# Moving one quad's copy, two tiles' normalisation and a send of weights between engines

## What is computed

```python
def _layernorm(x, g, b):
    m = x.mean(-1, keepdims=True)
    v = ((x - m) ** 2).mean(-1, keepdims=True)
    return (x - m) / jnp.sqrt(v + 1e-05) * g + b
def _attn(q_in, k_in, v_in, wq, bq, wk, bk, wv, bv, wo, bo, causal):
    ...
    scores = jnp.einsum('bqhd,bkhd->bhqk', Q, Kp) / jnp.sqrt(jnp.float32(HD))
    ...
    a = jax.nn.softmax(scores, axis=-1)
    o = jnp.einsum('bhqk,bkhd->bqhd', a, V).reshape(Bq, Sq, Dm)
    return o @ wo + bo
def _moe(x, rw, rb, w1, b1, w2, b2):
    router_weights = jax.nn.softmax(xf @ rw + rb, axis=-1)
    topw, topi = jax.lax.top_k(router_weights, K)
    ...
    out = jnp.einsum('etd,te->td', eo, combine)
x = _layernorm(x + _attn(x, x, x, ..., True), ln1_g, ln1_b)
x = _layernorm(x + _attn(x, encoder_output, encoder_output, ..., False), ln2_g, ln2_b)
x = _layernorm(x + _moe(x, router_w, router_b, e_w1, e_b1, e_w2, e_b2), ln3_g, ln3_b)
```

## Time and profile before

| | us |
|---|---|
| median of 3 runs | 758.14 |
| lowest, highest | 756.41, 762.37 |
| the profiled execution | 757.34 |
| its span in the profile | 755.6 |
| TensorE busy in it | 712.6 (94%) |
| VectorE busy | 498.8 (66%) |
| ScalarE busy | 369.4 (49%) |
| GpSimd busy | 286.9 (38%) |

### The profile page before, as it was taken

One profiled execution on the slowest core, in us unless ns is written; L12 is line 12 of the kernel. 1 busy time (PEld: TensorE's weight loads), 2 busy tenths in 40 slices (PEclk: granted clock), 3 DMA queues, 4 the chain that ended last, 5 costly groups with the idle time before them and its releaser, 6 DMA issues.

```text
span 755.6 us, 14560 instructions
## 1 busy us (share of the span) xinstructions
PE 712.6 (94%) x4969; PEld 478.9 (63%) x4969; DVE 498.8 (66%) x1376; ACT 369.4 (49%) x749; POOL 286.9 (38%) x558
## 2 busy tenths in 40 slices
PE   6889999999999999999997899999999999999983
PEld 4444434545464454645563586898999999999941
DVE  5679787678766877656668654465666665666436
ACT  4325465665666676667753446433433333333403
POOL 8305521543653463624653333212332332232114
PEclk9999999999999999999987999999999999999997
DMA  8964421343164021316016873677999999999654
GB/s 273 291 145 129 118 95 46 84 129 128 33 180 127 13 60 49 91 39 183 14 62 216 251 254 98 210 254 239 346 328 342 342 330 338 345 330 336 231 186 164
DMA packets 95154, 140.29 MB, mean 186 GB/s; under 512 B 11855, under 2 KB 81077, under 8 KB 92597
## 3 DMA queue, kind: packets, MB, share of 16 engines
q1 hardware_dynamic: 76357, 107.86, 45.3%
q10 hardware_dynamic: 15072, 22.02, 8.9%
q0 software_dynamic: 3648, 9.45, 3.4%
HBM read 110.65 MB, written 28.65 MB: 184 GB/s over the span
## 4 chain that ended last, share of the span: by engine, by line
PE 76%; DVE 8%; issue 8%; DMA 4%; POOL 2%; ACT 1%; DVEq 0%; SPq 0%; ACTq 0%; POOLq 0%
PE out_acc L984 12%; PE score_pair L961 10%; PE work L932 9%; PE score_pair L855 8%; PE work L849 8%; PE work L906 6%; PE work L855 4%; PE work L1008 4%; DVE neg_part_max L1472 3%; PE score_pair L849 3%; PE work L918 2%; PE work L992 2%; PE work L935 2%; DMA arena<-parts_scratch 1%; PE work L872 1%
## 5 line engine op out<-in xcount | busy, mean ns | idle before, releaser
L1472 DVE TENSOR_REDUCE neg_part_max<-work 128x1 f32<-128x512 f32 (+4 forms) x368 | 213.2, 625 | 66.8 <-PE work L935 36.1
L1244 ACT ACTIVATE arena<-score_pair 128x1024 f32<-128x1024 f32 (+2 forms) x224 | 178.7, 839 | 76.9 <-PE score_pair L961 75.7
L932 PE MATMUL work<-arena 96*128 96x77 bf16 (+4 forms) x640 | 118.2, 277 | 10.7 <-ACT arena L1207 2.7
L984 PE MATMUL out_acc<-arena 128*32 128x512 f32 (+4 forms) x896 | 103.7, 517 | 2.6 <-DVE arena L1492 2.6
L961 PE MATMUL score_pair<-arena 99*128 99x512 bf16 (+2 forms) x448 | 103.9, 337 | 1.0 <-ACT arena L1244 1.0
L1904 POOL DMA_INDIRECT chosen_scratch<-arena,scatter_rows x36 | 35.6, 989 | 174.8 <-DVE arena L1404 174.5
L855 PE MATMUL score_pair<-arena 128*128 128x256 f32 x432 | 97.6, 379 | 0.0
L932 PEld LDWEIGHTS work<-arena 96*128 96x128 bf16 x640 | 49.2, 98 | 74.7 <-issue 30.7
L1960 POOL TENSOR_SCALAR_AFFINE_SELECT arena<-arena 128x256 f32<-128x256 f32 x128 | 51.5, 410 | 118.0 <-ACT arena L1244 116.8
L1177 ACT ACTIVATE arena<-work,expert_b_cols 128x128 f32<-128x128 f32 x180 | 51.1, 369 | 84.2 <-PE work L849 79.4
L849 PE MATMUL work<-arena 128*128 128x128 f32 x720 | 87.2, 278 | 0.1
(11 more groups left out here) (257 smaller groups left out, 958.2 us busy)
## 6 DMA issues: line engine op xcount, KB each, us to landing
arena<-in_L_xattn_e_w SPq DMA_DIRECT2D x54, 1024.0 KB, 6.8
arena<-parts_scratch SPq DMA_DIRECT2D x24, 768.0 KB, 6.0
arena<-in_L_xattn_e_w ACTq DMA_DIRECT2D x18, 1024.0 KB
parts_scratch<-arena_more SPq DMA_DIRECT2D x24, 384.0 KB, 2.6
parts_scratch<-arena_more SPq DMA_DIRECT2D x24, 256.0 KB, 3.0
parts_scratch<-arena_more SPq DMA_DIRECT2D x24, 128.0 KB, 3.0
residual<-in_x SPq DMA_DIRECT2D x4, 512.0 KB, 8.0
tokens_scratch<-residual SPq DMA_DIRECT2D x2, 1024.0 KB, 4.8
```

What stands on the lines that cost most here:

```text
L932: m = pe.matmul(bank[:, j * it.w:(j + 1) * it.w], qa[st.half(it.g)][0:R_S, h, n0:n0 + P], k, start=True, stop=not it.last)
L984: m = pe.matmul(o_ps[c * VW:(c + 1) * VW, skip:QG], v, pt[buf][0:rows, j, 0:QG - skip], start=first, stop=last)
L1244: act_e.activation(pt[buf][0:rows, :, 0:w], st2[pair][0:rows, :, 0:w], ACT.Exp, scale=float(HD) ** -0.5).then_inc(pair_taken[pair], 1)
L1472: dve.tensor_reduce(pm[:, it.at, it.t, it.h0:it.h0 + it.nh], bank[:, 0:it.nh * it.w].rearrange("p (j k) -> p j k", j=it.nh), AX.X, ALU.max ...
```

## The change

Three things change; nothing else does.

1. A function `taken_by_scalar` decides who copies a quad. It differs from before for one quad: quad 0 of stage 7, half 0, is copied by ScalarE and no longer by VectorE.
2. A function `applied_by_pool` decides who normalises a tile. It differs from before for tiles 5 and 7 of sequence 1 after self-attention: ScalarE and GpSimd do them, in three instructions, and no longer VectorE, in two. TensorE's transposes of these two tiles wait for `normal_g` and no longer for `normal_v`; the counts that SyncE waits for at the end are adapted.
3. In `ORDER`, the `t_weights` of tile 0 (B) moves from before `w_exp` (X) to after that quad's `weigh` and `normalise`.

```diff
-    "R2q2M2Hewq2f2awlqsnqf2Pan2wn2q2n2Kywqfnf2qwfa2SRvhwuMRMRdMRMHt2yq2otoqtzwuvPKo2qSedwuq2Fq2BXwuawax2Oa2xBkxId"
+    "R2q2M2Hewq2f2awlqsnqf2Pan2wn2q2n2Kywqfnf2qwfa2SRvhwuMRMRdMRMHt2yq2otoqtzwuvPKo2qSedwuq2Fq2XwuBawax2Oa2xBkxId"
...
+def applied_by_pool(it):
+
+    return it.b == 0 or not it.cross and it.t in (5, 7)
+
+
+def taken_by_scalar(it):
+
+    return (it.g + it.quad) % 2 == 1 or (it.st.n, it.g) == (7, 0)
...
-            apply_n[it.cross, it.b, it.t] = sum(z.b == it.b for z in find("out_apply")[:it.n]) + 1
+            apply_n[it.cross, it.b, it.t] = sum(applied_by_pool(z) == applied_by_pool(it) for z in find("out_apply")[:it.n]) + 1
...
-        N_APPLY = 2 * TB
+        apply_at = {(it.cross, it.b, it.t): it.n for it in find("out_apply")}
+        N_BY_POOL = sum(applied_by_pool(it) for it in find("out_apply"))
+        N_BY_VECTOR = len(find("out_apply")) - N_BY_POOL
...
-            return (normal_v if b else normal_g, apply_n[cross, b, t])
+            by_pool = applied_by_pool(find("out_apply")[apply_at[cross, b, t]])
+            return (normal_g if by_pool else normal_v, apply_n[cross, b, t])
...
-                elif it.kind == "normalise" and (it.g + it.quad) % 2:
+                elif it.kind == "normalise" and taken_by_scalar(it):
...
-                elif it.kind == "out_apply" and it.b == 0:
+                elif it.kind == "out_apply" and applied_by_pool(it):
...
-                elif it.kind == "normalise" and (it.g + it.quad) % 2 == 0:
+                elif it.kind == "normalise" and not taken_by_scalar(it):
...
-                elif it.kind == "out_apply" and it.b == 1:
+                elif it.kind == "out_apply" and not applied_by_pool(it):
...
-                elif it.kind == "out_apply" and it.b == 0:
+                elif it.kind == "out_apply" and applied_by_pool(it):
...
-                    sp.wait_ge(normal_g, N_APPLY + (n + 1) * PIECE)
+                    sp.wait_ge(normal_g, N_BY_POOL + (n + 1) * PIECE)
                 else:
-                    sp.wait_ge(normal_v, N_APPLY + 1)
+                    sp.wait_ge(normal_v, N_BY_VECTOR + 1)
```

## The result

| | before | after |
|---|---|---|
| median of 18 runs each, us | 758.87 (756.41 to 765.10) | 763.34 (759.82 to 766.06) |
| ratio to before, with its 95% interval | 1 | 1.0052 [1.0036, 1.0069] |
| the profiled execution, us | 757.34 | 765.91 |
| its span, us | 755.6 | 764.2 |
| TensorE busy in it, us | 712.6 | 716.8 |

The change costs 2.7 to 5.2 us (the interval times 758.87). That is within 1%, and 763.34 lies inside the forecast range of 757.0 to 763.5, 0.2 under its upper end; the forecast was 760.1, a loss of about 2.4 us. The profiled execution of after is not a typical one: it lies 2.6 us above the median of its kernel. So the two spans, 8.6 us apart, must not be subtracted to get the price of the change.

What follows compares the result with a forecast made beforehand. TensorE bounds the kernel; copy, sends and tiles form one chain delaying the projection by 2.35 us, rounded to 2.4, giving 759.7 from the profiled execution or 760.5 from the median; forecast 760.1 us, range 757.0 to 763.5.

Steps and rivals of the forecast that it cites:

- The copy: Quad 0 of stage 7: ScalarE copies behind `w_exp` at about 407.4, so TensorE starts the next quad 0.35 us later.
- The sends: Two weight issues on ScalarE follow the copy, at 408.1 and 409.2; their lateness itself is priced at nothing.
- The tiles: Tiles 5 and 7 take 2.21 us each over ScalarE and GpSimd, against 1.00 on VectorE; tile 7's transposes +2.35 us.
- Tile 6: Before its transposes: VectorE has its data ready since 409, its two operations ending before tile 5 reaches GpSimd.
- GpSimd stretched: Rival at tiles 5 and 7: both GpSimd multiplies slowed by VectorE work, +0.86 us, so 761.0; chance 0.06.
- The clock: TensorE's granted clock, at its lower level from 405 us, came back at about 416, some 1.1 us into the projection.
- bounds of -0.5 and +2.7: Projections: gain about 0.5 us if the clock returns no later than before, +2.7 if only after both.
- The rival in which it lags through both projections: TensorE's clock stays at the lower level until both projections end: 760.1 + 2.7 = 762.8 us; chance 0.10.
- still at half behind 419: Sign that the forecast is wrong: TensorE's granted clock remains at half after 419 us.
- Behind the projection: Parts go out to HBM in 3.33 us and back in 5.51, unchanged, so the maxima are late with the projection.
- The early copy: Rival: ScalarE copies the quad at 405.1, projection gains 0.5 to 0.8 at full clock, 756.6 to 757.4; chance 0.12 shared with swallowed delay.
- likeliest case: The main forecast, projection and end 2.4 us late, 760.1 us, alone spanning 758.8 to 761.4; chance 0.69.

Runs made afterwards that it cites:

- copy alone: Kernel before with only the quad's copy moved to ScalarE; median 759.00 us, ratio 0.9992 [0.9968, 1.0017].
- sends back: Changed kernel with the two sends of weights put back ahead of `w_exp` on ScalarE; median 759.31 us, ratio 1.0023 [0.9994, 1.0052].
- copy early: Changed kernel with `w_exp` put behind the quad's copy and the sends behind `w_exp`; median 762.91 us, ratio 1.0055 [1.0034, 1.0076].
- everything early: Changed kernel with the copy, ScalarE's parts of tiles 5 and 7 and the sends all ahead of `w_exp`; median 758.71 us, ratio 0.9984 [0.9953, 1.0015].
- lean version: Changed kernel with copy, then sends, `w_exp` behind the last tile's transposes, all four tiles on VectorE; median 758.35 us, ratio 0.9998 [0.9976, 1.002].
- second set: The changed kernel run and profiled again with no edit; median 760.81 us, ratio to the kernel before 1.0034 [1.0015, 1.0053].
- tiles with sends: Changed kernel with the quad's copy back on VectorE; median 763.11 us, ratio 1.0041 [1.0016, 1.0065].
- only tile 5: Changed kernel with tile 7 back on VectorE, tile 5 staying on ScalarE and GpSimd; median 759.51 us, ratio 1.0002 [0.9976, 1.0028].
- copy with sends: Changed kernel with tiles 5 and 7 back on VectorE; median 760.32 us, ratio 1.0001 [0.9971, 1.0032].
- sends alone: Kernel before with only the two sends of weights moved behind `w_exp` and the quad; median 759.20 us, ratio 1.0013 [0.999, 1.0037].

## Why the prediction was right

**The copy.** Forecast: behind `w_exp`, 3.4 us after the start of the sums, with TensorE 0.35 us later than before. Measured: 3.33 (408.28 - 404.95) and +0.26; the copy took 0.57 us for the assumed 0.59, and started 0.11 us after the start of the second exponential instead of 0.17. This was the mechanism that the prediction turned on, and the trace has it as forecast. The copy alone gave +0.24 at tile 7.

**The sends.** Forecast from neighbours: first issue 0.68 us after the copy's start, the second 1.12 later. Measured: 0.77 and 1.12. The next instruction then follows 0.44 us after the second issue's start, so tile 5 starts 5.66 us behind the sums where the forecast had 5.3 to 5.6. It does not begin before the issue ends (0.39 us), as the lower bound had assumed.

**The tiles** were the term that was mis-sized. The price of 2.21 us (2.20 with the 0.72 that the earlier trace rows has for the add) ended with GpSimd's add and left out the hand-over to TensorE, 0.15 us; and tile 5's add took 0.80 instead of 0.72 or 0.73. From ScalarE's start to the transposes it was 413.04 - 410.61 = 2.43 us for tile 5 and 416.36 - 414.00 = 2.36 for tile 7. So TensorE waited 1.58 us before tile 5, not 1.1, and 1.73 before tile 7, not 1.6. Tile 5's transposes came at 8.09 for a forecast of 7.75 (+0.34), tile 7's at 11.41 for 11.03: +2.73 us against +2.35. The runs with one part undone show that it is this chain: with the sends back 1.82 us of it are gone, with tile 7 back on VectorE 1.94, and with the quad's copy early none of it but 0.18.

**Tile 6** was misread. The prediction has VectorE ready with it since 409, and its two operations over before tile 5 reaches GpSimd. But in VectorE's order the copy of tile 4's transposes stands ahead of tile 6, in the kernel before as well; the pair at 408.46 and 408.98 is tile 5's. The timeline of before, at 410 us:

```profile
410.28 0.42 DVE L1427 COPY arena_more<-work 128x256 f32<-128x256 f32 x1 [0.82 <-PE work L872]
...
410.62 0.47 DVE L1526 SCALAR_TENSOR_TENSOR residual<-residual,mean_var,param_rows 128x256 f32<-128x256 f32 x1
```

In the changed kernel the two operations of tile 6 ran at 411.83 and 412.35, right beside GpSimd's work on tile 5. This cost nothing, because they ended at 413.18 and TensorE came to tile 6 at 413.96.

**GpSimd stretched.** The rival's price went to the wrong engine. No GpSimd operation here took over 0.80 us; VectorE's were stretched instead, L1542 by 0.35 us (0.83 for 0.48) and L1720 by 0.40 (0.57, against 0.17 in the runs where no GpSimd instruction is beside it). SBUF — State Buffer of the Trainium skill (SBUF: two separate sides) states an exclusive lock between a GpSimd operation and a VectorE operation that has two SBUF inputs or runs in a 2-port mode: whichever starts first has it for its whole length, and the other is blocked. On VectorE's side the traces agree: L1720 ended at 416.24 and GpSimd's add at 416.21, L1542 at 413.18 and the add beside it at 412.89. On GpSimd's side they show less: its add at 412.09 took 0.07 us longer than usual, though VectorE's L1539 had begun before it and ran until 412.31. In the changed kernel this costs nothing: tile 6 waits for tile 5 and `rows` in TensorE's order anyway. In the version with everything early it held VectorE by 0.53, 0.47 and 0.35 us ahead of tile 4, of the 1.5 us by which tile 4 came later than expected.

**The clock.** The forecast kept the projection at its old length, with bounds of -0.5 and +2.7. It took 2.84 us for 2.48. The granted clock of the changed kernel, TensorE alone, from 417 us and from the start of the projection:

```profile
417.00:421.00 4.00, 4.00 (x13) 0.57 1.05 380
```

```profile
418.52:422.12 3.60, 3.60 (x11) 0.73 1.09 364
```

0.73 stands against 0.83 before. The maxima are 0.36 us later than tile 7's delay alone gives (3.09 - 2.73), which is the projection's 0.36. So the clock came back later than before by more than the work was moved, by a little, and neither bound was reached. The rival in which it lags through both projections did not happen. But one of the prediction's own signs of being wrong did: a granted clock "still at half behind 419". A mean of 0.57 from 417 to 421 us means the lower level until about 420.4, or 419.5 less the 0.95 us of offset. The clock came back 1.9 us into the first projection instead of 1.2; the second took 1.88 us, as before. So the sign came, and the large loss that it stood for did not. In the second execution of the changed kernel the clock came back 15.0 us behind the start of the sums instead of 15.5, the projection took 2.57 us, and the maxima were 2.61 us late.

**Behind the projection.** Forecast 3.33 + 5.51 us for the parts; 3.25 + 5.60 came, and TensorE's last wait, 1.31 us, is as before. The statement that a microsecond lost before the projection is a microsecond of the kernel fits the losses: +2.6 and +3.1 us at the maxima, 2.6 and 3.9 us by the ratios (0.34% and 0.52% of 759). For gains it was not seen: the lean version starts its projection 1.53 us earlier and its time cannot be told from before.

**The early copy** as a rival was priced at 756.6 to 757.4 if it happened. It did not happen, as forecast, and the lean version, where the copy is early, speaks against the price: 1.53 us of lead at the projection, 0.57 at the maxima, nothing in the time that the runs can tell ([-1.8, +1.5] us, which does not exclude it). In its trace the step that fails is "with the clock kept up the projection gains 0.5 to 0.8": the clock was not kept up (0.52), and the projection lost 1.1.

**How much of the hit is luck.** The place of the loss, its releasers and its size within 0.4 us at tile 7 were forecast. The time was not met as closely. The measured 763.34 lies above the likeliest case (758.8 to 761.4), and inside the range only through the room left for a clock that lags through both projections, which did not happen. Of the 3.2 us above the forecast, 1.1 are the kernel before, which the forecast took at 757.7 (between 757.34 and 758.14) and which was measured at 758.87; 0.4 are the tiles and 0.4 the projection. The remaining 1.4 or so are not traced to a place; the mean granted clock of the runs, 0.978 in this set and 0.980 in the second, hints at the clock and shows no more. The second set's 760.81 lies within the likeliest case.

**Open.** In the time from the parts' store to its landing there are two groups: 3.25 to 3.33 us in before, after, sends back, tiles with sends, copy alone, lean and only tile 5, and 3.9 to 6.2 in copy with sends, copy early, everything early and sends alone. The last has both its clock drop late and its store at 6.19 us. No single edit is common to the second group alone (after, tiles with sends, lean and only tile 5 have the sends moved too), and each value is from one execution. What decides it was not found.

## What to carry to other kernels

Before moving work to an engine that looks idle, read what it stands waiting for and what is queued ahead of the moved work: ScalarE was idle here only because it waited for VectorE's lists, and the issues of DMAs, 1.1 us apart, sit in the same queue. Price a hand-over between engines from the first engine's start to the consumer's start, not to the last producer's end. And judge two edits together, not each by itself: with the copy in place, the sends' move put tile 7 off by 0.02 us and the tiles' move by 0.67, and the two together by 2.49.

## What the runs showed of the hardware

- A gap that is closed need not pay. In the lean version's execution the projection was moved forward by 1.53 us, into TensorE's lower clock level, and took 3.60 us for 2.48 (granted 0.52 for 0.83). The length changes from execution to execution too: 2.84 and 2.57 us for the same kernel, and 2.33 to 3.60 over all thirteen.
- A GpSimd multiply or add of 128x256 can hold a short VectorE instruction with one input until it ends: a 128x16 operation of 0.17 us took 0.70 beside a multiply, and a 128x9 integer one 0.57 for 0.17. GpSimd's own operations, 0.72 or 0.73 us alone, took up to 0.90 in these stretches.
- An issue of a DMA of 1 MB by ScalarE, with the register loads ahead of it, put 1.12 us between two issues, and 0.44 us between the start of the last issue and the next instruction.
- One execution of the changed kernel had 4 us more behind the maxima than another of the same kernel, with the granted clock at 0.89 for 1.00 in two stretches of 15 us. What set it off is not known.
